# Heads layer of a graph network: node values spread to the edges by f32 products instead of bf16 parts

## The reference

```python
h_edge = ((atom[src] + bond) @ W).reshape(-1, H, D)
el = jnp.einsum('ehd,hd->eh', h_edge, attn_l)
er = jnp.einsum('nhd,hd->nh', h_node, attn_r)
s = el + er[dst]
s = jnp.where(s > 0, s, NEG_SLOPE * s)
smax = jax.ops.segment_max(s, dst, num_segments=N)
ex = jnp.exp(s - smax[dst])
denom = jax.ops.segment_sum(ex, dst, num_segments=N)
alpha = ex / denom[dst]
ft = jax.ops.segment_sum(h_edge * alpha[..., None], dst, num_segments=N)
```

## Time and profile before

| | us |
|---|---|
| median of 3 runs (8731.82 to 8734.40) | 8733.55 |
| the profiled execution | 8733.21 |
| its span in the profile | 8731.5 |
| busy: PE / PEld | 4763.8 / 4288.2 |
| busy: VectorE / ScalarE / GpSimd | 6710.5 / 4432.3 / 6328.2 |

### The profile page before, as it was taken

How to read it: one execution, slowest core, us unless ns; L and a number is a source line. 1 busy time by engine, 2 the same in 40 slices (tenths; PEclk the granted TensorE clock), 3 DMA queues, 4 the chain that set the end, 5 groups by cost and what they waited for, 6 DMA issues and landing times. The chain is left out here.

```text
span 8731.5 us, 120061 instructions
## 1 busy us (share of the span) xinstructions
PE 4763.8 (55%) x23534; PEld 4288.2 (49%) x23534; DVE 6710.5 (77%) x12205; ACT 4432.3 (51%) x11726; POOL 6328.2 (72%) x6675
## 2 busy tenths in 40 slices
PE   5777777777555555555545555555554444444444
PEld 5666666666444444444444444444443444444444
DVE  6888888888577777777767777777776777777777
ACT  5777777777444444444434444444443444444443
POOL 4777777777077777777767777777776777777776
PEclk8666666666655555555555555555555555555555
DMA  2222222222121222222212222222211222222221
GB/s 76 57 58 57 57 58 56 58 58 56 63 32 32 32 32 32 32 32 32 32 28 32 32 32 32 32 32 32 32 32 30 35 35 35 35 35 35 35 35 31
DMA packets 576283, 348.39 MB, mean 40 GB/s; under 512 B 451757, under 2 KB 452653, under 8 KB 576239
## 3 DMA queue, kind: packets, MB, share of 16 engines
q0 software_dynamic: 212992, 229.61, 16.3%
q1 hardware_dynamic: 362527, 118.16, 5.8%
q10 hardware_dynamic: 720, 0.17, 0.0%
HBM read 319.62 MB, written 27.76 MB: 40 GB/s over the span
## 5 line engine op out<-in xcount | busy, mean ns | idle before, releaser
L1610 POOL DMA_INDIRECT plain_rows_in<-table,plain_idx x4992 | 4723.7, 946 | 1523.8 <-issue 1523.2
L1858 PE MATMUL plain_ps_sums<-plain_rows_in,plain_prob 128*128 x10080 | 2298.8, 413 | 0.3 <-ACT plain_prob L1816 0.3
L1858 PEld LDWEIGHTS plain_ps_sums<-plain_rows_in,plain_prob 128*128 128x128 f32 x10080 | 2234.0, 330 | 27.8 <-ACT plain_prob L1816 0.9
L1029 POOL DMA_INDIRECT heads_rows_in<-h_in,heads_idx x1664 | 1590.7, 956 | 588.2 <-issue 507.4
L1816 ACT ACTIVATE plain_prob<-plain_prob 128x2048 f32<-128x2048 f32 x312 | 595.8, 1910 | 1969.7 <-DVE plain_prob L1742 1969.7
L1880 PE MATMUL plain_ps_max<-ident,plain_column_max 128*128 128x128 f32 x312 | 148.0, 474 | 1803.9 <-DVE plain_column_max L1722 1803.9
L1807 ACT ACTIVATE plain_ps_score<-plain_mask,plain_rows_in 128x128 f32<-128x128 f32 x3744 | 1110.9, 350 | 0.0
L1880 PEld LDWEIGHTS plain_ps_max<-ident,plain_column_max 128*128 128x128 f32 x312 | 56.9, 182 | 1895.7 <-DVE plain_column_max L1722 1895.7
L1742 DVE TENSOR_TENSOR plain_prob<-plain_prob,plain_ps_max 128x2048 f32<-128x2048 f32 x312 | 714.0, 2288 | 267.5 <-PE plain_ps_max L1885 267.5
L1664 DVE SCALAR_TENSOR_TENSOR plain_mask<-plain_mask,plain_ps_er 128x2048 f32<-128x2048 f32 x315 | 720.6, 2287 | 193.0 <-PE plain_ps_er L1833 192.8
L1807 ACT ACTIVATE plain_score_sb<-plain_mask,plain_rows_in 128x128 f32<-128x128 f32 x1248 | 398.5, 390 | 902.6 <-DMA plain_rows_in<-table,plain_idx 902.6
(11 more groups left out here) (250 smaller groups left out, 8659.5 us busy)
## 6 DMA issues: line engine op xcount, KB each, us to landing
plain_rows_in<-table,plain_idx POOLq DMA_INDIRECT x4992
heads_edges<-in_edge_attr SPq DMA_DIRECT2D x108, 512.0 KB
heads_rows_in<-h_in,heads_idx POOLq DMA_INDIRECT x1664
plain_own<-table SPq DMA_DIRECT2D x324, 33.5 KB, 2.3
table<-plain_out_sb SPq DMA_DIRECT2D x208, 33.5 KB
plain_idx<-in_src SPq DMA_DIRECT2D x324, 8.0 KB
plain_dst_ids<-in_dst SPq DMA_DIRECT2D x324, 8.0 KB
plain_unit_par<-unit_floats SPq DMA_DIRECT2D x324, 1.0 KB
```

Source lines behind the costliest of these rows:

```text
L1029: gp.indirect_dma_start(rows_in[h][:, t, :], None, table[:, :], bass.IndirectOffsetOnAxis(ap=idx[h][:, t:t + 1], axis=0)).then_inc(gathere ...
L1610: gp.indirect_dma_start(rows_in[h][:, t, :], None, table[:, :], bass.IndirectOffsetOnAxis(ap=idx[h][:, t:t + 1], axis=0)).then_inc(gathere ...
L1858: ins = te.matmul(sums[h % 2], prob[h % 2][:, t, :], rows, start=t == 0, stop=t == Q - 1)
```

## The change

`node_vals` is used as it is, in f32, and so is the turned one-hot. The three parts, the tiles that held them (`rest`, `node_split`) and the sum of the parts are gone. `edge_vals` is now a view of the PSUM bank into which the products write, and the two logit steps that use it read it there. The signal `split_made` becomes `maxima_made` and is given one step after the maxima, not after the split. The carried maximum sits at another place of the same bank. VectorE's count of chained steps per unit falls from 24 to 19.

```diff
-    PARTS = 3
-    MAX_IN_AT = Q * PARTS * vals
+    MAX_IN_AT = Q * vals
-        onehot_t = [sb(f"onehot_t{k}", [NB, CAP], BF16) for k in range(2)]
+        onehot_t = [sb(f"onehot_t{k}", [NB, CAP]) for k in range(2)]
-        rest = sb("rest", [NB, vals])
-        node_split = sb("node_split", [NB, PARTS, vals], BF16)
-
-        edge_vals = sb("edge_vals", [P, Q, vals])
+        edge_vals = ps_edge[:, 0:Q * vals].rearrange("p (t k) -> p t k", k=vals)
...
-                    step(ve.tensor_tensor(node_vals[:, heads:vals], max_before[:, :], max_unit[:, :], ALU.max))
-
-                    step(ve.tensor_copy(node_split[:, 0, :], node_vals[:, :]))
-                    step(ve.tensor_tensor(rest[:, :], node_vals[:, :], node_split[:, 0, :], ALU.subtract))
-                    step(ve.tensor_copy(node_split[:, 1, :], rest[:, :]))
-                    ve.tensor_tensor(node_split[:, 2, :], rest[:, :], node_split[:, 1, :], ALU.subtract
-                                     ).then_inc(split_made, 1)
+                    ve.tensor_tensor(node_vals[:, heads:vals], max_before[:, :], max_unit[:, :], ALU.max
+                                     ).then_inc(maxima_made, 1)
+                    ve.wait_ge(maxima_made, n + 1)
...
                     ve.wait_ge(expanded, n + 1)
-                    step(ve.tensor_reduce(edge_vals[:, :, :], ps_edge[:, 0:Q * PARTS * vals]
-                                          .rearrange("p (t s k) -> p t k s", s=PARTS, k=vals), AX.X, ALU.add))
...
-                        te.wait_ge(split_made, n + 1)
+                        te.wait_ge(maxima_made, n + 1)
                         for t in range(Q):
-                            te.matmul(ps_edge[:, PARTS * vals * t:PARTS * vals * (t + 1)],
-                                      onehot_t[h % 2][:, t * P:(t + 1) * P],
-                                      node_split[:, :, :].rearrange("p s k -> p (s k)"))
+                            te.matmul(edge_vals[:, t, :], onehot_t[h % 2][:, t * P:(t + 1) * P], node_vals[:, :])
```

More of the change, by code:

```diff
@@ L911, in heads_layer @@
             sem("masked_made"), sem("columns_maxed"), sem("maxima_turned"))
-        split_made, expanded, logits_made, weights_made, rescaled = (
-            sem("split_made"), sem("expanded"), sem("logits_made"), sem("weights_made"), sem("rescaled"))
+        maxima_made, expanded, logits_made, weights_made, rescaled = (
+            sem("maxima_made"), sem("expanded"), sem("logits_made"), sem("weights_made"), sem("rescaled"))
         rows_weighted, aggregated, acc_carried = sem("rows_weighted"), sem("aggregated"), sem("acc_carried")
@@ L1042, in _ @@
                 rounds = unit_rounds(ve)
-                STEPS = 24
+                STEPS = 19
                 for h in range(RING):
```

## The result

The changed kernel takes 9090.55 us (4 runs, 9088.62 to 9094.22), the kernel before 8732.95 us beside it: ratio 1.041, 95% interval 1.0395 to 1.0425. It is slower by 358 us. The forecast was 9045 us, in a range of 8940 to 9130.

The account below looks back on a forecast made before the run. VectorE's ordered list of steps was taken as the bound, 20.48 us a unit. A later first logit step, 3.57 us, less 0.57 for high-clock starts, gave 3.0 us x 104 = 312 us, so 9045 us; range 8940 to 9130.

Parts of the forecast that it names:

- What bounds it: Heads layer: VectorE's ordered list is the path at 20.48 us a unit; GpSimd's gathers are a floor at 20.18.
- faster rival: Spread done before VectorE finishes weighing, under 0.075 us a piece; GpSimd then bounds, 8703 us; chance 0.03.
- What goes: On VectorE: four split steps, 0.81 us, and the reduction over parts, 0.38 us, go; together 1.19 us a unit.
- What comes: TensorE's f32 spread, 34 pieces with the carried maximum: first logit step 3.57 us later at low clock, 0.26 at high.
- Which clock: TensorE's spread runs at its starting clock; one unit in four starts high, saving 0.57 us on the mean.
- rival with the lifted clock: Clock rises inside TensorE's spread some 5 us after its start: 2.35 us a unit, 245 us, 8978 us; chance 0.29.
- What else moves: ScalarE's projection copy stays hidden by 0.1 us, TensorE's room before its next turn stays, f32 copies and GpSimd's waits cost nothing.

Follow-up runs that it names:

- e10: Kernel before, its three bf16 products of a tile added up in PSUM, without VectorE's sum over the parts: ratio 0.9992, 8734.69 against 8742.45 us.
- e4: Changed kernel with the four steps of the split put back on VectorE, their result unread: ratio 1.0264 to the kernel before.
- e8: Same kernel as e4, run once more: changed kernel with the four unused split steps back on VectorE; ratio 1.0259 to the kernel before.
- e11: Changed kernel with only the first 8 of the spread's 16 products, in a call of its own: 8751.15 us, ratio 1.0018 to the kernel before.
- e2: Changed kernel with the one-hot in bf16 and node values rounded to one bf16 part: ratio 0.9938, 11694.67 against 11768.89 us of the kernel before.
- e3: Changed kernel with 12 filler turns of the identity on TensorE before the spread: ratio 1.0351 to the kernel before.
- e12: Same kernel as e3, in a call of its own: 12 filler turns before the spread; 8971.77 us, ratio 1.0278 to the kernel before.
- e6: Same kernel as e11, an earlier run: changed kernel with 8 of the spread's 16 products; ratio 0.9963 to the kernel before.

## Why the prediction was right, step by step

- **What bounds it.** Right. VectorE's list was the path, and what was put in front of L1142 lengthened every unit. GpSimd's floor existed, as e10 shows, but at 20.42 us when VectorE runs close behind the gathers, not at 20.18. The faster rival's 8703 us was out of reach even with a free spread in three parts; I had taken the gathers' pace at a time at which they ran ahead.
- **What goes.** The four steps and the reduction are gone, and L1121 (the old L1128) starts 0.20 us behind the start of L1118. The gain was hidden by the wait, as e4 and e8 show. PSUM reads cost nothing: L1142 takes 0.19 us as L1151 did.
- **What comes.** 32 pieces, as L1314 had said. The low-clock unit is longer by 7.51 - 3.79 = 3.72 us, forecast 3.57. The distance of two pieces is (3.58 - 0.35) / 15 = 0.215 us in e11, where L1314's merged row had given 0.204, and 34 pieces multiply that. The high-clock start costs 5.07 - 3.79 = 1.28 us, forecast 1.3.
- **Which clock.** Right in kind: a spread that began at 0.50 stayed there to its end in all 91 units, although TensorE was busy throughout, and in the 13 that began at 1.00 the clock fell to 0.50 after 2.65 to 2.85 us, as forecast (2.85). The rival with the lifted clock (8978 us) falls. Wrong in size: 13 of 104 units had the high start, not one in four. That is the larger part of the 45 us missed: 13 units by 2.4 us, 32 us. With both corrected, (91 x 3.72 + 13 x 1.28) / 104 = 3.42 us a unit; measured 23.89 - 20.48 = 3.41.
- **What else moves.** Right that nothing there costs time, wrong in one reason. ScalarE's L1237 ended at 1021.17, 0.10 us before the end of VectorE's last logit step. GpSimd stands still between units, at no cost. But "everything shifts alike, so that room stays" does not hold, even by my own numbers: the end of the spread moves from 1011.27 to 1016.61, 5.3 us, and VectorE by 3.57. So TensorE's room ahead of its next turn had to shrink. In the unit shown it is 0.73 us where it was 3.73. Over 300 to 2100 us it is 220.9 / 88 = 2.5 us a unit before and 61.8 / 75 = 0.8 us after, under 0.1 us in 20 of those 75 units:

```profile
PE heads_ps_turn L1325 <- ACT heads_pairs_t L1208: 220.9, 88, 4.0
...
PE heads_ps_turn L1316 <- ACT heads_pairs_t L1199: 61.8, 47, 2.5
```

The first line is of the kernel before, the second of the changed one (us in total, times, longest). It cost nothing, as the rest of the unit, 16.69 us, shows; but a much longer spread would have had little room left there.

What stays open: why the share of high starts was an eighth. In the kernel before the clock was at 1.00 when the node values were ready in 26 of 104 units, just the one in four that I took; in the changed kernel in 13. So the change itself moved the share. That it depends on how the unit's length and the clock's changes fall together is my guess; no run shows it. Open is also whether the f32 weights or the f32 columns make the pieces dear, since e2 changes both.

## What to carry to other kernels

When a step is moved from one type to another, price it by a row of the same shape and type in the same trace, count the pieces that the trace has for it, and price it at the clock that is granted at its place, not at the mean; then ask how much cover it has: here 1.2 us of saved VectorE steps met a spread that grew from 0.6 to 7.0 us with 2.5 us of cover. And a floor that an engine shows while it runs ahead is not the floor that it has when its consumer runs close behind.

## What the runs showed of the hardware that I had not expected

On two chips TensorE's instructions came late. In e3, turns of the identity that wait for nothing, rows of the timeline:

```profile
1003.36 0.27 PE L1353 MATMUL heads_ps_scores<-ident 128*128 128x128 f32 x1 [0.39 <-issue]
1004.10 0.30 PE L1353 MATMUL heads_ps_scores<-ident 128*128 128x128 f32 x1 [0.47 <-issue]
1006.19 0.37 PE L1353 MATMUL heads_ps_scores<-ident 128*128 128x128 f32 x1 [1.79 <-issue]
1007.62 0.37 PE L1353 MATMUL heads_ps_scores<-ident 128*128 128x128 f32 x1 [1.05 <-issue]
1010.44 0.37 PE L1353 MATMUL heads_ps_scores<-ident 128*128 128x128 f32 x1 [2.45 <-issue]
```

They stand 0.7 to 2.8 us apart, where in e12 twelve of them take 1.51 us. VectorE, ScalarE and GpSimd had such gaps too, up to 15.2, 15.0 and 17.2 us in e3's heads layer. The kernel before was 35% slower there, and what an edit was worth changed with it: e6 was faster than the kernel before (0.9963), e11, the same kernel, slower (1.0018). The Trainium skill (Runtime: NRT & Kernel Launch, "Instruction fetch mechanics") says that instructions are fetched by DMA in blocks and that a taken branch can force a fetch; whether that is what was slow here, no run tells. The other thing is the clock: TensorE was busy for 6.7 us on end in the spread and the clock stayed at 0.50.
